# Another slot for eight pieces of work around the attention scores of a two-layer transformer block with routed experts

## The reference

```python
# layer 0: attention with 16 heads of 16, modulated by a condition vector c (8 x 64)
attn = softmax(q @ k.T / 4)                      # per head, 512 x 512
coh  = sigmoid(tanh([x, c] @ Wc1.T + bc1) @ Wc2.T + bc2)
mod  = attn * coh; mod = mod / (mod.sum(-1) + 1e-8)
mod  = 0.79 * mod + 0.21 * fa                    # fa: softmax over positions, from c alone
x    = x + (mod @ v) @ Wout.T + bout
# layer 1: 8 experts, each token's two best by a gate
gate = softmax(rms_norm(x) @ wg + wg_b + c @ gg + gg_b); cw = the two largest, zero elsewhere
h1 = relu(x @ W1[e] + b1[e]); h2 = relu(h1 @ W2[e] + b2[e])
x  = x + sum over e of cw[e] * (h2 @ W3[e] + b3[e])
```

## Time and profile before

| | us |
|---|---|
| median of 3 runs | 940.82 (937.77 to 941.13) |
| the profiled execution | 950.3 |
| its span, first to last instruction | 948.4 |
| TensorE matmul busy | 878.1 (93%) |
| VectorE busy | 699.8 (74%) |
| ScalarE busy | 581.5 (61%) |
| POOL busy | 406.3 (43%) |
| maxima on VectorE (512) | 324.3 |
| exponentials on ScalarE (512) | 277.4 |

### The profile page before, as it was taken

One profiled execution on the slowest core, in us unless ns is written; L12 is line 12 of the kernel. 1 busy time (PEld: TensorE's weight loads), 2 busy tenths in 40 slices (PEclk: granted clock), 3 DMA queues, 4 the chain that ended last, 5 costly groups with the idle time before them and its releaser, 6 DMA issues.

```text
span 948.4 us, 23132 instructions
## 1 busy us (share of the span) xinstructions
PE 878.1 (93%) x6806; PEld 514.9 (54%) x6807; DVE 699.8 (74%) x1680; ACT 581.5 (61%) x1256; POOL 406.3 (43%) x446
## 2 busy tenths in 40 slices
PE   5799999999999999998888989799999999999994
PEld 2232333333333333332231678678888888888873
DVE  6768889888998988989996387768865555555442
ACT  3147877877778878787586657655444444444441
POOL 4313435555646656553253326643553233223322
PEclk9679999999999999999896899989999999999998
DMA  6543243443526426171053187875644333333432
GB/s 207 121 80 71 66 53 91 97 113 79 97 82 109 122 60 127 42 124 48 13 173 114 26 243 179 192 191 100 129 74 57 46 57 52 51 46 55 66 49 25
DMA packets 109434, 88.36 MB, mean 93 GB/s; under 512 B 63816, under 2 KB 102216, under 8 KB 107024
## 3 DMA queue, kind: packets, MB, share of 16 engines
q1 hardware_dynamic: 95664, 68.05, 31.6%
q0 software_dynamic: 13296, 18.23, 11.6%
q10 hardware_dynamic: 384, 0.93, 0.3%
HBM read 44.97 MB, written 33.31 MB: 83 GB/s over the span
## 4 chain that ended last, share of the span: by engine, by line
PE 74%; DVE 11%; ACT 5%; DMA 4%; issue 3%; POOL 1%; SPq 1%; DVEq 0%; ACTq 0%; POOLq 0%
PE bank L1053 30%; PE bank L950 10%; PE bank L898 10%; PE bank L1069 9%; PE bank L885 8%; DVE mx L1320 5%; PE bank L874 4%; ACT arena L1203 2%; PE bank L956 2%; DVE arena L1627 1%; DMA w_b<-mxp 1%; PE bank L1008 1%; DMA out<-y,y_dest 1%; POOL arena L654 1%; ACT arena L1151 1%
## 5 line engine op out<-in xcount | busy, mean ns | idle before, releaser
L1320 DVE TENSOR_REDUCE mx<-bank 128x1 f32<-128x512 f32 x512 | 324.3, 682 | 49.2 <-PE bank L874 46.1
L1203 ACT ACTIVATE arena<-bank 128x512 f32<-128x512 f32 x512 | 277.4, 596 | 70.4 <-PE bank L885 68.5
L1239 ACT ACTIVATE hf<-bank,small 128x256 f32<-128x256 f32 (+1 forms) x312 | 133.5, 456 | 190.2 <-PE bank L1053 188.3
L753 POOL DMA_INDIRECT out<-y,y_dest x71 | 130.5, 1838 | 239.5 <-DVE y_dest L1608 207.8
L1053 PE MATMUL bank<-hh,arena 128*128 128x256 f16 (+1 forms) x1248 | 198.6, 265 | 0.1
L874 PE MATMUL bank<-arena 48*128 48x512 f16 x512 | 170.8, 396 | 16.8 <-DVE mx L1320 12.8
L1589 DVE TENSOR_TENSOR hl<-hf,hh 128x256 f16<-128x256 f32 (+1 forms) x304 | 112.6, 395 | 93.7 <-ACT hh L1243 93.2
L885 PE MATMUL bank<-arena 49*128 49x512 f16 x512 | 164.5, 394 | 14.6 <-DMA arena<-w_b 6.3
L1053 PE MATMUL bank<-hl,arena 128*128 128x256 f16 (+1 forms) x624 | 163.6, 263 | 0.0
L898 PE MATMUL bank<-arena 128*17 128x512 f32 x1024 | 139.6, 618 | 0.9 <-ACT arena L1203 0.9
L885 PEld LDWEIGHTS bank<-arena 49*128 49x128 f16 x512 | 39.1, 94 | 177.5 <-ACT arena L1203 149.2
(11 more groups left out here) (228 smaller groups left out, 971.3 us busy)
## 6 DMA issues: line engine op xcount, KB each, us to landing
raw<-in_we SPq DMA_DIRECT2D x16, 1024.0 KB, 5.2
arena<-parts_dram SPq DMA_DIRECT2D x84, 128.0 KB
parts_dram<-arena SPq DMA_DIRECT2D x64, 128.0 KB, 1.8
arena<-in_xT SPq DMA_DIRECT2D x8, 512.0 KB, 4.5
arena<-in_x SPq DMA_DIRECT2D x8, 512.0 KB, 5.9
out<-rows SPq DMA_DIRECT2D x8, 512.0 KB, 5.2
xs<-in_pads SPq DMA_DIRECT2D x9, 272.0 KB, 3.6
arena<-parts_dram SPq DMA_DIRECT2D x24, 64.0 KB, 3.0
```

The lines of the kernel that those rows point to most:

```text
L753: pool.indirect_dma_start(out=out, out_offset=bass.IndirectOffsetOnAxis(ap=y_dest[:, par, s:s + 1], axis=0), in_=y[:, par, s, :], in_offse ...
L1203: nc.scalar.activation(pr[:, s % TT, n, :], b_bank[no % B_RING][:, :], ACT.Exp, scale=SCALE).then_inc(b_read, 1)
L1239: nc.scalar.activation(hf[which][:, m, 0:n], layer[which][m // 2][:, m % 2 * TS:m % 2 * TS + n], ACT.Relu, bias=bias[which][:, bass.ds(e, ...
L1320: V.tensor_reduce(mx[:, g % 2, c, s % TT:s % TT + 1], a_bank[no % A_RING][:, :], X, ALU.max).then_inc(a_read, 1)
```

## The change

Eight pieces of work are moved to other slots; no instruction is added or taken away. The v product 0 goes from slot 0 to slot 4, the v sum from 7 to 6 (POOL's part of it from 6 to 5), turning 0 from slot 11 to slot 0 of the next batch (in the last batch to slot 13), v product 2 from 14 to 13 and projection 3 from 13 to 14, with the write of its parts and the stack read behind it. The x parts are made in slots 1 (ScalarE) and 2 (POOL) in place of 4 and 5. The squares of row blocks 0 to 3 stand in slots 5, 5, 6, 7 in place of 4, 5, 6, 7. The high row parts go from slots 8 and 9 to 6 and 9, the low ones from 8 and 10 to 7 and 14, and the targets of the scatters from 14 to 15.

```diff
 PLAN = {
-    0: [("coh", 0, 0), ("v", 0, 1)],
+    0: [("at", 0, -1), ("coh", 0, 0)],
...
-    4: [("op", 1, -1)],
+    4: [("op", 1, -1), ("v", 0, 1)],
     5: [("ot", 0, 0), ("op", 2, -1)],
-    6: [("op", 3, -1)],
-    7: [("vs", 0, 0), ("c1", 0, 1)],
+    6: [("op", 3, -1), ("vs", 0, 0)],
+    7: [("c1", 0, 1)],
...
-    11: [("at", 0, 0), ("v", 1, 1)],
+    11: [("v", 1, 1)],
     12: [("pj", 1, 2), ("count", 0, -1)],
-    13: [("ot", 2, 0), ("pj", 3, 2)],
-    14: [("v", 2, 1)],
+    13: [("ot", 2, 0), ("v", 2, 1)],
+    14: [("pj", 3, 2)],
...
-SENT_AT = {8: 0, 10: 1}
+SENT_HIGH_AT = {6: 0, 9: 1}
+SENT_AT = {7: 0, 14: 1}
+SQUARES_AT = {5: (0, 1), 6: (2,), 7: (3,)}
...
-STACKS_AT = {0: 0, 3: 1, 4: 2}
+STACKS_AT = {1: 0, 3: 1, 4: 2}
...
-PARTS_AT = (10, 12, 14, 15)
+PARTS_AT = (10, 12, 14, 16)
...
+    if s == FINAL + 13:
+        here.append(("at", 0, B - 1))
...
+            if at == PARTS_AT[3] - SLOTS and 0 <= b + 1 < B:
+                write_parts(3, b + 1)
...
-            if at in PARTS_AT and 0 <= b + 2 < B:
+            if at in PARTS_AT[:3] and 0 <= b + 2 < B:
                 write_parts(PARTS_AT.index(at), b + 2)
...
-            if at == 5 and 0 < b + 2 < B:
+            if at == 2 and 0 < b + 2 < B:
                 split_x(b + 2)
-            if at == 6 and 0 <= b < B:
+            if at == 5 and 0 <= b < B:
                 sum_values(b)
...
-            if at == 14 and 0 <= b - 1 < B:
+            if at == 15 and 0 <= b - 1 < B:
                 targets(b - 1)
...
-            if 4 <= at < 8 and 0 <= b - 1 < B:
-                square_rows(at - 4, b - 1)
-            if at in (8, 9) and 0 <= b - 1 < B:
-                send_high(at - 8, b - 1)
+            if at in SQUARES_AT and 0 <= b - 1 < B:
+                for t in SQUARES_AT[at]:
+                    square_rows(t, b - 1)
+            if at in SENT_HIGH_AT and 0 <= b - 1 < B:
+                send_high(SENT_HIGH_AT[at], b - 1)
...
-            if at == 4 and 0 < b + 2 < B:
+            if at == 1 and 0 < b + 2 < B:
                 split_x(b + 2)
```

## The result

The changed kernel takes 964.2 us (median of 4 runs, 962.8 to 968.3) where the kernel before takes 941.0 (4 runs, 937.8 to 947.0): 1.025 times as long, interval 1.019 to 1.031. The prediction was 957, between 938 and 975. Some executions of the kernels further down were in a slower state of the chip: the medians and ratios leave these out, and of the traces only that of the run with the late subtraction is of such an execution, whose clock in batches 1 to 5 is full.

The account below looks back on a forecast made before the run. TensorE, busy 55.73 of 57.26 us a batch, sets the pace. Gains -1.8, wait +3.2 and clock +1.6 make +3.0 in each of batches 2 to 6; in all +16.6 on the median 940.8: 957 us, range 938 to 975.

Parts of the forecast that it names:

- The wait of `send_high`: Slot 6: ScalarE waits for the last scatter to land, so TensorE stands still 3.2 us a batch (1.7 to 5.3).
- The clock: Behind TensorE's standstill in slot 6 the granted clock falls to half speed, costing 1.6 us a batch.
- The gains, -1.8 a batch: Moved work shortens slots 4 to 7 and 11 to 12, less a cost in slot 0: -1.8 us a batch.
- slots 11 and 12, -1.3: Turning 0 leaves slot 11 and VectorE reaches slot 12 earlier: -1.3 us, between 0.5 and 1.8.
- slots 4 to 7, -0.7: Late exponentials and waits go, a v product enters slot 4: 14.57 us become 13.9, if ScalarE is free.
- turning 0 in slot 0, +0.3: Its subtraction waits for ScalarE's copy and delays VectorE's work in slot 1: +0.3 us, between 0 and 0.7.
- Batch 6: Forecast like batches 2 to 5: gains, scatter wait in slot 6 and half clock, together +3.0 us.
- Batch 7: Has the wait and clock loss in an already waiting slot, none of the gains, and turning 0 twice: +4.6 us.
- The base: Profiled execution before took 950.3 us, 9.5 above the runs' median 940.8; the forecast difference was added to the median.
- (a): Rival: the scatter wait in slot 6 is hidden and only the gains stay, -10.7, 930 us; chance 0.09.
- (b): Rival: the scatter wait in slot 6 is short (1.7 us) and the clock holds, 938 us; chance 0.10.
- (c): Rival: the slot 6 wait is 5.3 us, or scatters take 8.2 as in the expert stage: 970 or 986; chance 0.17.

Follow-up runs that it names:

- the run with the late subtraction: Changed kernel with the first high parts in slot 7, and GpSimd's split of slot 10's projection moved behind the two marks in slot 12: 942.0 us.
- x part back: Changed kernel with the high parts in slot 8, and the x part returned from slots 1 and 2 to slots 4 and 5: 947.9 us.

## Why the prediction was right, and where it was not

*The wait of `send_high`: right in place, cause and sign.* Counted from the start of slot 4 (305.42) it forecast the last scatter at 8.9, its landing at 12.4 and ScalarE at 8.9. Measured: 9.64, 12.39 and 9.84. The landing fits because two errors of 0.7 cancel: the scatter starts later, and takes 2.75 rather than 3.5. ScalarE waits 2.55 (3.5 forecast), TensorE 2.24 (3.2).

*The clock:* 1.6 forecast, about 2.0 measured (slot 7 is 5.04 against 3.46 in batch 4 with the high parts in slot 8, slot 8 3.99 against 3.55). Wait and clock are 4.2 together in this batch, where the sum had 4.8. Over batches 2 to 5 slots 6 to 8 are 15.17 for 10.39 with the high parts in slot 8, so 4.8 on the average: this term of the sum was right.

*The gains, -1.8 a batch: this is the step that failed.* With the wait undone batches 2 to 5 take 57.3, and 57.6 before: 0.2 a batch. Even that is mostly one wait in the trace before, in batch 2, of a score tile of slot 8 for the turned maxima:

```profile
202.06 0.37 PE L885 MATMUL bank<-arena 49*128 49x512 f16 x1 [1.49 <-DMA arena<-w_b]
```

Of the waits of that kind, which the prediction named as a sign against it, the changed kernel has 0.3 us in batches 2 to 5, the kernel before 2.0. The terms of the gain:
- slots 11 and 12, -1.3: mis-sized, -0.59 measured (8.35 to 7.76; slot 12 is 4.81, forecast 3.8), near the 0.5 that the prediction gave as the least. I took TensorE's wait for the thing to remove. VectorE, busy 4.71 of the 4.92 us of slot 12 before, seems to set the end of slot 12 through its chain to the count (with one step of it 0.8 shorter slot 12 fell by 0.3, as the run with the late subtraction shows), and part of its earlier start went into waiting for GpSimd.
- slots 4 to 7, -0.7: right only where the scatters come early. With GpSimd's x part in slot 7 slots 4 to 7 are 13.8 (6.95 + 3.29 + 3.60) against 14.57. In the changed kernel slot 4 is 4.2, not 3.7 (slot 5 is 3.6, forecast 3.4). I had seen that GpSimd's x part goes ahead of the scatters of slots 3 and 4, and asked only when they land.
- turning 0 in slot 0, +0.3: +0.32 measured. Slots 13 to 15, priced at nothing: +0.3, and back to 10.36 with the old order.

*Batch 6* had the wait (slot 6 is 5.57, before 2.94), but no half clock behind it, and its last slots were shorter; it lost nothing where +3.0 was forecast. In the kernel before the clock stood at 0.50 in its slots 13 and 15 (from 449.5 and, as in the earlier trace rows, from 459.75), after not; why it held there was not tried. *Batch 7* came out at the forecast +4.6, which proves little: it also took 77.1 in the run with the high parts in slot 8.

*The base.* The forecast for the batches was +16.3, the traces give +17.7; the medians differ by 23.2. That the sums of the batches agree is luck: batches 2 to 5 lie 5.6 above their forecast together, batch 6 lies 3.9 below. Ahead of batch 0 and behind batch 7 the trace after is 3.5 us shorter. What is missing is mostly the profiled execution before, which stands 9.3 above its median. In which stretch, the traces don't show; the start of batch 0 alone lies between 50.0 and 56.3 in those that I read it from.

*The rivals.* (a) falls, the wait was there; (b) falls, it was longer than 1.7 and the clock fell; (c) falls, the scatters landed 2.75 us after their issue, not 8.2.

## What to carry to other kernels

Before moving a step earlier, look for the newest write or read it has to wait for, and who issues that: a step that never waits in its old place may have only a few microseconds of room (here one slot: 7 is free, 6 costs 20 us). Where an engine's wait is to be removed, ask whether the engine it waits for has idle time at all; if not, only that engine's own work counts. And a standstill of TensorE cost here nearly as much again in the slots behind it, at half clock.

## What was not expected of the hardware

*VectorE waits for GpSimd, to the end of its instruction.* A comparison of 128x32 takes 0.18 alone and 1.02, 0.70 or 0.51 beside a GpSimd instruction, with which it ends within 0.05 us (276.17 and 276.12; 273.32 and 273.28). The same holds for the split of the maxima (137.80 and 137.76). The Trainium skill states it in SBUF — State Buffer, section Who interferes with whom: a VectorE instruction with two inputs in SBUF, or in one of its two-port modes, and a GpSimd instruction that reads SBUF exclude each other, and the later one waits until the first is done. The traces here agree. VectorE's reductions from the banks went on beside GpSimd at their usual 0.6 to 0.7 each.

*Products of TensorE end late without a record of it.* In slot 4 of the changed kernel ScalarE starts 1.3 us after the end of the last record of the product that it waits for; in slot 5 of the run with all scatters in slot 4 it is 2.1 us (309.57, the v product's records end at 307.46), and TensorE itself stands still for 1.00. It goes from slot 4 when the scatters come earlier (x part back, GpSimd's x part in slot 7). Without the stack reads it is still there, in part in slot 5. The runs tie it to GpSimd's scatters beside the products; the mechanism stays open.
